# A six-layer transformer kernel: the norms that stand alone ahead of an expert layer done by halves of the tokens, each half followed by its routing

## The reference, cut to what matters

```python
x = x + 0.5 * _L0_ffn_ref(_layernorm(x), ...)   # top1
x = x + _L0_attn_ref(_layernorm(x), ...)
x = x + 0.5 * _L0_ffn_ref(_layernorm(x), ...)   # top1
x = x + 0.5 * _L1_ffn_ref(_layernorm(x), ...)   # top4
x = x + _L1_attn_ref(_layernorm(x), ...)
x = x + 0.5 * _L1_ffn_ref(_layernorm(x), ...)   # top4

def _L1_ffn_ref(x, router_w, router_bias, ...):
    logits = flat @ router_w.T + router_bias
    scores = softmax(logits)
    topk_scores, topk_idx = top_k(scores, 4)
    topk_scores = topk_scores / topk_scores.sum(-1)
    h = silu(flat @ gate_w[e]) * (flat @ up_w[e])      # for each expert e
    out = sum over the four of topk_scores * (h @ down_w[e])
    return out + silu(flat @ sgate) * (flat @ sup) @ sdown
```

## Time and profile before

| | |
|---|---|
| median of 3 runs | 2139.44 us (2139.2 to 2139.88) |
| the profiled execution | 2136.94 us, of which the span 2135.2 us |
| busy in the span | DVE 68%, PE 59%, ACT 47%, POOL 42% |
| chain of waits that ended last | DVE 26%, POOL 20%, PE 15%, DMA 12%, ACT 9%, issue 16% |
| its largest lines | L620 on POOL (the sends) 10%, L971 on POOL (the gathers) 9% |

### The profile page before, as it was taken

The page is one execution under the profiler, slowest core; times in us unless marked ns, Lnnn a source line. Parts: engine busy times, 40 slices in busy tenths (PEclk is TensorE's granted clock), DMA queues, the critical chain, the costliest instruction groups (busy, mean ns, idle before and its releaser), DMA issues.

```text
span 2135.2 us, 43776 instructions
## 1 busy us (share of the span) xinstructions
PE 1260.7 (59%) x15168; PEld 937.5 (44%) x15169; DVE 1457.0 (68%) x3558; ACT 993.4 (47%) x1825; POOL 893.1 (42%) x1015
## 2 busy tenths in 40 slices
PE   2176388898836731674772337777786245838351
PEld 1066377777726620264660113444443113727320
DVE  6667589999875788443464658989897963626352
ACT  3354366776624530343341226888888222514220
POOL 0703300000023334655456635667665066545564
PEclk9998599999958965988885665555555577969775
DMA  4522420000002210153551100000000012626312
GB/s 158 198 66 67 178 101 1 0 0 0 1 14 78 79 28 27 46 170 125 164 157 43 45 23 1 2 2 2 2 1 2 4 46 85 205 85 188 96 48 72
DMA packets 78330, 139.49 MB, mean 65 GB/s; under 512 B 15744, under 2 KB 32768, under 8 KB 76928
## 3 DMA queue, kind: packets, MB, share of 16 engines
q1 hardware_dynamic: 57728, 95.89, 13.5%
q0 software_dynamic: 20480, 41.98, 6.7%
HBM read 67.56 MB, written 70.25 MB: 65 GB/s over the span
## 4 chain that ended last, share of the span: by engine, by line
DVE 26%; POOL 20%; issue 16%; PE 15%; DMA 12%; ACT 9%; DVEq 0%; SPq 0%; ACTq 0%; POOLq 0%
POOL slots_top L620 10%; POOL AREA L971 9%; DMA slots_top<-XH,ROW 6%; ACT AREA L1267 5%; DMA AREA<-results_top,ROW 4%; PE PS L285 3%; DVE AREA L1333 2%; PE PS L287 2%; PE PS L286 2%; PE PS L1508 2%; DVE AREA L1320 2%; DVE AREA L942 2%; DVE AREA L1674 2%; DVE AREA L390 2%; PE PS L1524 1%
## 5 line engine op out<-in xcount | busy, mean ns | idle before, releaser
L620 POOL DMA_INDIRECT slots_top<-XH,ROW x320 | 333.3, 1041 | 694.1 <-DVE ROW L574 520.9
L971 POOL DMA_INDIRECT AREA<-results_top,ROW x320 | 314.9, 984 | 353.7 <-DMA results_top<-AREA 151.0
L946 DVE TENSOR_TENSOR AREA<-AREA 128x512 f16<-128x512 f32 (+1 forms) x144 | 125.8, 873 | 122.9 <-ACT AREA L914 122.1
L914 ACT ACTIVATE AREA<-AREA 128x512 f16<-128x512 f32 (+1 forms) x144 | 111.2, 772 | 173.6 <-DVE AREA L938 98.8
L1469 POOL TENSOR_TENSOR AREA<-AREA 128x1024 f16<-128x1024 f32 x64 | 151.3, 2363 | 92.7 <-ACT AREA L1609 92.5
L818 PE MATMUL PS<-IDH,AREA 128*128 128x128 f16 x960 | 82.8, 230 | 166.3 <-DMA AREA<-slots_top 155.5
L1698 DVE TENSOR_REDUCE AREA<-PS 128x4 f32<-128x1024 f32 x128 | 156.1, 1219 | 31.0 <-PE PS L1496 30.4
L1602 ACT ACTIVATE AREA<-PS,AREA 128x1024 f32<-128x1024 f32 x128 | 142.5, 1114 | 54.1 <-PE PS L1508 54.0
L927 DVE COPY AREA<-PS 128x1024 f16<-128x1024 f16 (+1 forms) x144 | 85.6, 594 | 115.0 <-PE PS L818 114.9
L818 PEld LDWEIGHTS PS<-IDH,AREA 128*128 128x128 f16 x960 | 63.2, 103 | 174.3 <-DMA AREA<-slots_top 160.4
L421 PE MATMUL PS<-IDH,XH 128*128 128x128 f16 x384 | 47.9, 310 | 154.2 <-DVE XH L397 154.2
(11 more groups left out here) (273 smaller groups left out, 5293.0 us busy)
## 6 DMA issues: line engine op xcount, KB each, us to landing
AREA<-slots_top SPq DMA_DIRECT2D x96, 256.0 KB
results_top<-AREA SPq DMA_DIRECT2D x96, 256.0 KB
slots_top<-ZERO SPq DMA_DIRECT2D x2, 6144.0 KB, 26.6
AREA<-slots_top SPq DMA_DIRECT2D x48, 128.0 KB
results_top<-AREA SPq DMA_DIRECT2D x48, 128.0 KB
slots_top<-XH,ROW POOLq DMA_INDIRECT x320, 2.2
AREA<-results_top,ROW POOLq DMA_INDIRECT x320
slots_top<-ZERO SPq DMA_DIRECT2D x2, 1536.0 KB, 13.3
```

Of the source, the lines that this page charges most:

```text
L620: nc.gpsimd.indirect_dma_start(out=L.xs[q], out_offset=bass.IndirectOffsetOnAxis(ap=ROW[:, n:n + 1], axis=0), in_=XH[:, t * 2 * D:(t + 1) ...
L946: nc.vector.tensor_tensor(HH[1][:, v, :HCOL], HF[:, v, :HCOL], HH[0][:, v, :HCOL], ALU.subtract).then_inc(bl_lo.sem, 1)
L971: nc.gpsimd.indirect_dma_start(out=YG[:, g % 2, c * D:(c + 1) * D], out_offset=None, in_=L.ys[g * GT // L.tiles], in_offset=bass.IndirectO ...
```

## The change

ln_scalar, ln_vector and ln_tensor take the part q and do four of the eight groups; ln_vector computes the scales of the 16 tiles of that part alone. route_scalar, route_vector and route_tensor take q as well. The engines' programs call them in turn: norm of part 0, routing of part 0, norm of part 1, routing of part 1. The statistics, the sends, SP's waits and the weights are left as they are.

```diff
-        def ln_vector(dve, first, link):
-            if first:
+        def ln_vector(dve, first, link, q):
+            if first and q == 0:
                 with dve.Fori(0, NG) as g:
                     for j in range(GT):
                         statistics(g * GT + j)
             dve.wait_ge(*consts.at(CONSTS))
-            dve.wait_ge(*ln_stat.at(NT))
-            ln_scales(link, 0, NT)
-            for g in range(NG):
+            dve.wait_ge(*ln_stat.at((q + 1) * NT // 2))
+            ln_scales(link, q * NT // 2, (q + 1) * NT // 2)
+            first, last = q * NG // 2, (q + 1) * NG // 2
+            for g in range(first, last):
                 ln_center(dve, g)
-                if g > 0:
+                if g > first:
                     ln_rest(dve, g - 1)
-            ln_rest(dve, NG - 1)
+            ln_rest(dve, last - 1)
...
-        def ln_tensor(pe, L):
-
-            if L:
-                pe.wait_ge(*w_lo.at(FIRST if L is L0 else len(splits)))
-            for g in range(NG):
+        def ln_tensor(pe, L, q):
+
+            pe.wait_ge(*w_lo.at(FIRST if L is L0 else len(splits)))
+            first, last = q * NG // 2, (q + 1) * NG // 2
+            for g in range(first, last):
                 ln_transpose(pe, g)
-                if L and g > 0:
+                if g > first:
                     ln_logits(pe, L, g - 1)
-            if L:
-                ln_logits(pe, L, NG - 1)
+            ln_logits(pe, L, last - 1)
...
-        def route_vector(dve, L):
-            link = Chain(dve, rt_step)
+        def route_vector(dve, L, q):
+            link = Chain(dve, rt_step, q * route_steps(L) // L.parts)
             if L is L1:
                 dve.wait_ge(*bias_loaded.at(16))
-            for q in range(L.parts):
-                dve.wait_ge(*logits.at((q + 1) * NG // L.parts))
-                route_part(dve, L, q, link)
-            assert link.n == route_steps(L)
+            dve.wait_ge(*logits.at((q + 1) * NG // L.parts))
+            route_part(dve, L, q, link)
+            assert link.n == (q + 1) * route_steps(L) // L.parts
...
                 if ready:
                     for s, c in ready:
                         dve.wait_ge(s, c)
-                    ln_vector(dve, n == 0, norm_link)
                 k = n + 1 if nxt else None
                 if ph in ("moe0", "moe1"):
                     L = L0 if ph == "moe0" else L1
-                    route_vector(dve, L)
+                    for q in range(L.parts):
+                        if ready:
+                            ln_vector(dve, n == 0, norm_link, q)
+                        route_vector(dve, L, q)
                 if n == 0:
                     split_vector(dve, FIRST, len(splits))
```

More of the change, by code:

```diff
@@ L449, in ln_scalar @@
-        def ln_scalar(act):
-            for g in range(NG):
+            ln_rest(dve, last - 1)
+        def ln_scalar(act, q):
+            first, last = q * NG // 2, (q + 1) * NG // 2
+            for g in range(first, last):
                 ln_half(act, g)
-                if g > 0:
+                if g > first:
                     ln_copy(act, g - 1)
-            ln_copy(act, NG - 1)
-        def ln_tensor(pe, L):
-            if L:
-                pe.wait_ge(*w_lo.at(FIRST if L is L0 else len(splits)))
-            for g in range(NG):
+            ln_copy(act, last - 1)
@@ L461, in ln_tensor @@
+        def ln_tensor(pe, L, q):
+            pe.wait_ge(*w_lo.at(FIRST if L is L0 else len(splits)))
+            first, last = q * NG // 2, (q + 1) * NG // 2
+            for g in range(first, last):
                 ln_transpose(pe, g)
-                if L and g > 0:
+                if g > first:
                     ln_logits(pe, L, g - 1)
-            if L:
-                ln_logits(pe, L, NG - 1)
+            ln_logits(pe, L, last - 1)
         LN_COUNTS = {ln_stat: NT, ln_norm: NG, ln_hi: NG, ln_lo: NG, ln_tr: NG, ln_xt: NG}
-        def route_tensor(pe, L):
-            for q in range(L.parts):
[L473 to L482, removed]
@@ L484, in route_vector, with route_tensor @@
-        def route_vector(dve, L):
-            link = Chain(dve, rt_step)
+        def route_tensor(pe, L, q):
+            pe.wait_ge(*rt_choice.at(q + 1))
+            wait(pe, rt_row, q)
+            n = L.ET
+            nc.tensor.matmul(banks(4)[:, :n], TRI[:, :], MH[:, :n], start=True, stop=True)
+            nc.tensor.matmul(banks(6)[:, :n], ONES[:, :], MH[:, :n], start=True, stop=True
+                             ).then_inc(rt_pos.sem, 1)
+            pe.wait_ge(*rt_bex.at(q + 1))
+            wait(pe, rt_tab, q)
+            nc.tensor.transpose(banks(5)[0:1, 0:P], BEX[:, :], IDF[:, :]).then_inc(rt_brow.sem, 1)
@@ L596, in route_steps, with route_scalar @@
             return L.parts * (5 + (0 if L.K == 1 else 2) + 3 + 5 + 2 + 2 + 2 + 2 * L.K + 5 + (7 if L is L1 else 0))
-        def route_scalar(act, L):
+        def route_scalar(act, L, q):
             if L is L1:
                 ex = EX[:, :L.ET]
-                for q in range(L.parts):
-                    for n, v in enumerate((ex, W4[:, q * L.tiles:(q + 1) * L.tiles, :])):
-                        act.wait_ge(*rt_shift.at(2 * q + n + 1))
-                        nc.scalar.activation(v, v, ACT.Exp).then_inc(rt_exp.sem, 1)
+                for n, v in enumerate((ex, W4[:, q * L.tiles:(q + 1) * L.tiles, :])):
+                    act.wait_ge(*rt_shift.at(2 * q + n + 1))
+                    nc.scalar.activation(v, v, ACT.Exp).then_inc(rt_exp.sem, 1)
         def carry_wait():
@@ L1842, in run @@
                     L = L0 if ph == "moe0" else L1
-                    route_scalar(act, L)
+                    for q in range(L.parts):
+                        if ready:
+                            ln_scalar(act, q)
+                        route_scalar(act, L, q)
                 if n == 0:
@@ L1903, in run @@
                     L = L0 if ph == "moe0" else L1
-                    route_tensor(pe, L)
+                    for q in range(L.parts):
+                        if ready:
+                            ln_tensor(pe, L, q)
+                        route_tensor(pe, L, q)
                     if L is L1:
```

3 lines of the change are left out of this document (removed).

## The result

| | before | after |
|---|---|---|
| median | 2139.88 us of 9 runs (2137.5 to 2144.14) | 2145.7 us of 9 runs (2144.34 to 2152.25) |
| the profiled execution | 2136.94 us | 2147.18 us |
| its span | 2135.2 us | 2144.7 us |

The ratio is 1.0031, with a 95% interval of 1.0018 to 1.0043: slower, by 3.9 to 9.2 us.

The account below looks back on a forecast made before the run. The prediction took DVE's weight splits to bound the first layer, the sends of part 0 the third, and POOL the sixth. +10.0 - 1.3 - 4.0 = +4.7 on 2139.44 gave 2144.1 us, range 2141.0 to 2148.4.

Parts of the forecast that it names:

- Half of the norm, 14.2 us: On DVE, scales 3.62, four groups fewer 7.81 and the added wait 2.78 make 14.2 us for each half.
- ROW 4.5 earlier: Slot numbers of part 0, which start its sends, come 4.5 us earlier: 18.7 - 14.2.
- routing end 9.7 later: DVE's routing of both parts ends 9.7 us later: 2 x 14.2 - 18.7.
- tail without cover: At the end of each half DVE waits for the last group's router products, 2.78 us more.
- First layer +10.0: DVE's splits of the weights start 9.7 later, plus 0.3, delaying the load of slots; bounds 7.7 to 11.
- allowance of 0.3 for scales beside sends: In the first layer, part 1's scales run beside POOL's sends; one slowed instruction is 0.25 us, 0.3 added.
- Rival 1: First layer: the weights' chain takes back 2 us, total +2.7, 2142.1 us; chance 0.15.
- Third layer -1.3: Load of slots goes out at 645.4 instead of 646.67, bound by DVE's routing, no longer sends; bounds -1.6 to 0.
- Sixth layer -4.0: Sends of part 0 start 4.5 us earlier, less 0.5 for one send held beside the norm of part 1.
- Rival 2: Sends are held beside the norm by 4.5 us, so the sixth layer gains nothing: +8.7, 2148.1 us; chance 0.12.
- Rival 3: First layer bound by the weights' DMA, absorbing the late start of splits: -5.3, 2134.1 us, faster; chance 0.07.
- Rival 4: Sixth layer's sends don't start earlier, tied to something else; no gain anywhere, +10.0, 2149.4 us; chance 0.04.

Follow-up runs that it names:

- e1: Norm by halves in the first layer alone, against the kernel before: 2148.19 us against 2139.56, ratio 1.0051.
- e2: Norm by halves in the sixth layer alone, against the kernel before: 2136.59 us, ratio 0.9995.
- e3: Norm by halves in the third and sixth layers, first as before, against the kernel before: 2135.35 us, ratio 0.9981.
- e9: Norm whole; in the first layer three large weight splits moved between the two routing parts, against the kernel before: 2137.79 us against 2141.05, ratio 0.9980.
- e10: Third and sixth layers halved, scales once; first-layer early splits: two before routing, three between routings; against the kernel before: 2138.90 us against 2144.91, ratio 0.9970.
- e5: Third and sixth layers halved, with part 1's remainder (L397) on one column of each group; run once for its trace, 2132.72 us.
- e6: Third and sixth layers halved, with part 1's centring (L390) on one column of each tile; run once for its trace, 2135.14 us.

## Why the prediction was right

- **Half of the norm, 14.2 us; ROW 4.5 earlier; routing end 9.7 later.** First scales to L508 in the changed kernel: 35.66 - 21.43 = 14.23. ROW of part 0 came 4.5 earlier in the third layer (first send 25.76 behind the scales, where it was 30.27) and 4.3 in the sixth. Each tail without cover showed 2.73 to 2.82 us of idle time, 2.78 forecast.
- **First layer +10.0.** The splits started 9.93 later and the load of slots came 9.54 later (e1: 9.41). Of the allowance of 0.3 for scales beside sends 0.15 is there: 46.44 to 50.21 is 3.77 where the half without sends took 3.62 (21.43 to 25.05). Rival 1, in which the weights' chain gives 2 back, isn't seen: from the first split to the load it is 36.7 us in the changed kernel and 36.5 in e1, and 37.1, 37.5 and 36.4 in before, e2 and e3, whose first layer is the same. In the reason for it the forecast misread a row: a send is 32 packets, so the 480 of the earlier trace rows are 15 sends and not 16 of 30. That moves nothing.
- **Third layer -1.3.** -1.25 and -1.27, and SP's last wait there is the one for DVE, as named. But the margin was thinner than forecast: the sends had landed 1.4 us ahead of DVE's step (the wait for L572 above) and not 3.2 (642.2 and 645.4), because four of them were held beside the norm, 1.9 us in all. The forecast counted such holds in the sixth layer and left them out here; DVE's later end covered them.
- **Sixth layer -4.0: the mis-sized term.** The gain of 4.5 came as 4.3 to 4.4. Against it I had set 0.5 for held sends, from a count of four remainders and one hit. The holds beside the norm were 0.25 + 0.48 = 0.73 in e3, which is near. But the sends of part 0 lasted 3.0 to 3.2 longer. In e3 the 3.24 are mostly 2.05 from the wait for landing and 1.14 of holds, of which 0.4 lies beside the routing of part 1, where sends fall on other instructions than before. The forecast had a price for a held send and none for the wait behind every eighth, which ends with the slowest of 16 DMA engines. In e3 the layer gave 1.95 instead of 4.0. In the profiled execution of the changed kernel it gave -4.32 + 3.02 + 1.50, so nothing. The 1.50 of part 1 lies almost wholly in the waits for landing (31.8 us in all, where they were 30.4). It is in none of e1 to e9, but e10 has 1.20; what makes these waits differ from one execution to the next is open.
- **Sum.** By the changed columns of e1 and e3 the parts are +9.4 - 1.3 - 2.0 = +6.1, where the forecast had +4.7; the medians are 5.8 apart. The spans of the two profiled executions are 9.5 apart, 1.0 of that in stretches that didn't change. That the sum is off by no more is in part luck: the forecast had the sixth layer 2.0 too good and the first 0.6 too bad. The margin was small too, since the forecast lay 0.4 above its own bound for slower.
- **The rivals.** Rival 2 (sends held beside the norm) is half true: the price of 4.5 us, where it would have eaten the whole gain, wasn't reached in e2 or e3, and the larger part of what was lost is not a hold. The prediction misread one row for it: the send of 7.10 us in the earlier trace rows met three splits of 2.2 us, two of FC and one of PJ, and not two. Rival 3 (the first layer bound by the weights' DMA) fell with e1, and e9 shows the grain of truth in it: started earlier, the same row of splits does run into the DMAs. Rival 4 fell with the first send.

## What to carry to other kernels

Cutting a step in halves moves the first result forward and the last one back; price both, and look in each place which of the two the next stage waits for, since the same edit was worth +9.5, -1.3 and -2 us in three layers of one kernel. An uncovered tail (here 2.8 us of transposition, copy and products) is paid once for every piece. Where an earlier start leads into a row of round trips through a few buffers, look at how many pieces the buffers let run ahead: here three early splits on three slots brought the end 3.6 us forward, and not the 10.8 of the start.

## What the runs showed of the hardware

- An indirect DMA on POOL that starts 0.05 to 0.54 us behind the start of a 0.69 us DVE instruction with two SBUF inputs ends 0.83 to 0.84 us behind the end of that instruction, and beside a long row of them likewise: in the changed kernel 7.24 us beside three splits of the weights (start 72.21, 0.84 behind their end at 78.61). One that starts ahead of the instruction, by as little as 0.03 us, isn't held.
- The other way round, a float32 `TENSOR_SCALAR` of 128x128 in SBUF that falls on the end of a send took 0.39 to 0.56 us where it takes 0.32 to 0.35, and ended 0.02 to 0.03 us behind the send (24 of them).
- Held sends can lock into step with a DVE loop of the same period (1.75 us here).
- One packet of instructions took 0.96 to 1.5 us on one of the 16 DMA engines. Where it came between the packets of a send, the wait for landing took 3.5 to 3.7 us instead of 1.53 (three executions); where it came behind them, 1.53 (e5, e6).
